# A graph layer and a slice-attention layer: identity matmuls added to TensorE's block loop

## The reference, cut to what matters

```python
# x: 6250 x 256; 106250 edges sorted by dst; all float32
edge_index = jnp.stack([src, dst])
# 1. graph layer on layernorm(x), 256 -> 256
support = x @ W
r_D = jax.nn.sigmoid(support @ a2)
gated = r_D * support
out = segment_sum(gated[col] * edge_values[:, None], row)     # row = src, col = dst
sumnorm = segment_sum(edge_values * r_D[col, 0], row)
out = out / sumnorm[:, None]
out = elu(max(out, 0) + softplus(out @ a1) * min(out, 0))
x = x + out
# 2. slice attention on layernorm(x), 8 heads, 64 slices of 64 channels
slice_weights = softmax((x_mid @ W_slice + b_slice) / temp)    # per node and head, over 64 slices
slice_token = einsum('bhnc,bhng->bhgc', fx_mid, slice_weights) / (slice_norm + 1e-5)
out_slice = softmax(q @ k.T * SCALE) @ v                       # tiny: 64 tokens per head
out_x = einsum('bhgc,bhng->bhnc', out_slice, slice_weights)
x = x + (out_x @ W_out + b_out)
```

## Time and profile before

| what | value |
|---|---|
| time, median of 3 runs | 1913.37 us (1912.43 to 1913.96) |
| time of the profiled execution | 1912.43 us |
| its span | 1910.5 us |
| PE busy | 1414.9 us (74%) |
| DVE busy | 1096.4 us (57%) |
| POOL busy | 902.8 us (47%) |
| ACT busy | 310.4 us (16%) |
| mean granted TensorE clock | 0.771 of full speed |

### The profile page before, as it was taken

How to read it: one execution, slowest core, us unless ns; L and a number is a source line. 1 busy time by engine, 2 the same in 40 slices (tenths; PEclk the granted TensorE clock), 3 DMA queues, 4 the chain that set the end, 5 groups by cost and what they waited for, 6 DMA issues and landing times.

```text
span 1910.5 us, 24715 instructions
## 1 busy us (share of the span) xinstructions
PE 1414.9 (74%) x6339; PEld 1032.4 (54%) x6340; DVE 1096.4 (57%) x2743; ACT 310.4 (16%) x800; POOL 902.8 (47%) x922
## 2 busy tenths in 40 slices
PE   4488877776588776777677876677776787777898
PEld 3477777775255444544445554445544454445687
DVE  8999999996344545444444454444444444444422
ACT  0022222222001111111111111111111111111133
POOL 0121111111666666666666666666666666665000
PEclk8688888887677777777777777677777777777899
DMA  7000000002633333333333333333333333333012
GB/s 205 2 22 20 20 20 20 20 20 34 103 94 86 88 82 86 88 85 88 88 85 91 88 85 86 88 90 88 85 85 86 90 87 86 92 84 84 26 63 71
DMA packets 92334, 139.42 MB, mean 73 GB/s; under 512 B 43147, under 2 KB 63007, under 8 KB 92312
## 3 DMA queue, kind: packets, MB, share of 16 engines
q0 software_dynamic: 42800, 114.46, 22.5%
q1 hardware_dynamic: 49512, 24.69, 4.8%
HBM read 123.65 MB, written 15.43 MB: 73 GB/s over the span
## 4 chain that ended last, share of the span: by engine, by line
PE 28%; issue 28%; DVE 26%; DVEq 6%; ACT 4%; another core or an unknown queue 3%; DMA 2%; POOL 1%; SPq 1%; ACTq 0%; POOLq 0%
PE bank L1261 27%; DVE big L667 6%; DVE big L677 5%; DVE S L932 3%; DVEq L82 1%; DVEq L932 1%; POOL rows L590 1%; DMA res<-in_x_dram 1%; DVE big L686 1%; PE bank L1310 1%; DVE big L656 1%; ACT xn L1203 1%; DVE lg L980 1%; ACT neg L1196 1%
## 5 line engine op out<-in xcount | busy, mean ns | idle before, releaser
L590 POOL DMA_INDIRECT rows<-gated_rows_dram,ring_i x857 | 825.6, 963 | 468.5 <-issue 228.4
L1261 PE MATMUL bank<-rows,S 128*128 128x257 f32 (+1 forms) x2156 | 621.0, 436 | 172.8 <-issue 159.0
L1261 PEld LDWEIGHTS bank<-rows,S 128*128 128x128 f32 x2156 | 464.1, 221 | 323.7 <-issue 237.4
L932 DVE TENSOR_SCALAR S<-iota,lof,srec 128x128 f32<-128x128 f32 x882 | 245.7, 359 | 101.0 <-issue 38.4
L1261 PE MATMUL bank<-big 128*98 128x80 f32 (+2 forms) x1741 | 220.0, 303 | 84.8 <-DVE big L699 84.8
L1261 PEld LDWEIGHTS bank<-big 128*98 128x98 f32 (+1 forms) x1741 | 215.3, 221 | 86.2 <-issue 86.2
L523 POOL DMA_INDIRECT sorted_edges_dram<-big,idx x52 | 74.8, 1439 | 389.4 <-ACT big L1114 278.3
L979 DVE TENSOR_REDUCE hm<-bank 128x8 f32<-128x512 f32 x49 | 33.9, 692 | 312.2 <-PE bank L1261 199.3
L1261 PE MATMUL bank<-Wxs,xT 128*128 128x512 f32 x196 | 181.1, 1079 | 5.2 <-ACT xT L1210 5.2
L1310 PE MATMUL bank<-ident,xn 128*128 128x128 f32 x98 | 32.0, 427 | 174.5 <-ACT xn L1203 141.0
L667 DVE TENSOR_TENSOR big<-big 128x784 f32<-128x784 bf16 x104 | 152.7, 1530 | 0.0
(11 more groups left out here) (209 smaller groups left out, 1217.3 us busy)
## 6 DMA issues: line engine op xcount, KB each, us to landing
rows<-gated_rows_dram,ring_i POOLq DMA_INDIRECT x857
gated_rows_dram<-S SPq DMA_DIRECT2D x49, 128.5 KB
res<-in_x_dram SPq DMA_DIRECT2D x1, 6144.0 KB
out_dram<-S SPq DMA_DIRECT2D x48, 128.0 KB, 1.7
sorted_edges_dram<-big SPq DMA_DIRECT2D x2, 465.5 KB, 7.2
sorted_edges_dram<-big,idx POOLq DMA_INDIRECT x52, 2.3
srec<-sorted_edges_dram SPq DMA_DIRECT2D x2, 374.0 KB
srec<-in_L_ffn_W_x_dram SPq DMA_DIRECT2D x2, 256.0 KB
```

Of the source, the lines that this page charges most:

```text
L590: pool.indirect_dma_start(rows[:, u, :], None, gtab[:, :], bass.IndirectOffsetOnAxis(ap=ring_i[:, k, u:u + 1], axis=0)).then_inc(s_row[u], 16)
L932: v.tensor_scalar(S[:, u, :], iota[:, :], lof[:, k, u:u + 1], srec[:, 1, ds(b * TQ + u, 1)], ALU.is_equal, ALU.mult).then_inc(s_S, 1)
L1261: return nc.tensor.matmul(o, l, r, start=start, stop=stop, skip_group_check=True)
```

## The change: identity matmuls in the block loop

A helper `idle(n)` is added in TensorE's program. It multiplies the identity by itself n times into columns 256 to 383 of `bank[6]`, with no wait and no semaphore. One such product follows each of the row tiles 4 to 9, and eight stand ahead of the transposes of each block but the last, which keeps its `spin(8)`. The first row tiles of block 0, which are done ahead of the loop, get the six too.

```diff
@@ segment(b, k, lo, hi, start=False)
                     mm(bank[k][:, 0:GW], S[:, u, :], rows[:, u, :], u == 0, u == TQ - 1).then_inc(s_seg, 1)
+                    if 4 <= u < 10:
+                        idle(1)
+
+            def idle(n):
+                for _ in range(n):
+                    mm(bank[6][:, F:F + P], ident[:, :], ident[:, :])
@@ main(b, k, left, start=False, second=False)
                 if left:
                     segment(b + 1, 1 - k, 4, 10)
-                if not left:
+                if left:
+                    idle(8)
+                else:
                     spin(8)
                 transposes(b + NB, xn[:, :], bank[6][:, 0:F])
```

## The result

| | before | changed |
|---|---|---|
| median, 4 runs each | 1913.66 us (1912.43 to 1916.32) | 2015.04 us (2006.90 to 2015.55) |
| ratio, 95% interval | | 1.0518 (1.0489 to 1.0547) |
| profiled span | 1910.5 us | 2004.9 us |
| mean granted clock | 0.771 | 0.826 |
| a pass of two blocks | 52.69 us | 56.56 us |

I had predicted 1864 us, faster. The clock came up as foreseen, and the kernel got slower all the same. The difference of the spans, 94.4 us, lies in the block loop. In the changed kernel the transposes of block 1 start at 562.08 and those of block 47 at 1863.05: 1300.97 us against 1211.91, 89 us more in 23 passes, and 9 more up to block 1, 4 less behind.

A forecast was written before the change was run, and what follows sets the result against it. TensorE's clock, falling in waits for `xn`, was taken to delay GpSimd's eleventh gather, with GpSimd's own time the floor. 80% of 2.55 us, 2.0 us x 24 passes = 49 us, gave 1864 us; range over the cases 1838 to 1935.

The forecast's parts named there:

- the clock behind the wait: TensorE behind the short block's wait for `xn`: windows would read 0.9 or more in place of 0.51.
- TensorE's wait for `xn`: Ahead of the transposes, 3.6 us each in 36 waits: the products would shrink it to under 1 us.
- the way to row tile 12: From the transposes through the logits: 4.69 us at full clock against 7.91, so 3.2 us less per block.
- the long block: Longer block of a pass: transposes 1.5 us late, row tile 14 done 2.2 us sooner, against 2.38 us to gain.
- the slow stretch: Long block until 1050.94, engines but GpSimd issuing slowly: bounded by time, so added products partly take row tiles' place in it.
- The last term: From `xn` to the transposes: 1.5 us late in the longer block, bounds 0 to 3.3; clock kept in the other.
- the short one: Shorter block of a pass: 3.3 us of products fit the 3.6 to 3.8 us wait at no cost.
- The floor: GpSimd's own time for a two-block pass: 50.14 us, 2.55 under today's 52.69.
- The other two: GpSimd's stops of 2.3 and 4.3 us at the starts of a pass's two blocks, taken as its own cost.
- D: Rival, chance 0.04: slow stretch goes by instructions at 0.70 us each, 14 us a pass, 336 us slower, 2249.
- A: Rival, chance 0.17: longer block's transposes 3.3 us late and cold, logits still 7.9 us, 79 us slower, 1992.
- C: Rival, chance 0.07: GpSimd's 4.3 and 2.3 us stops wait for TensorE; freed, 109 us faster, 1804.

The follow-up runs named there:

- e7: The changed kernel with the gathers of odd row tiles left out from block 1 on: 1645.2 us, 0.860 of the kernel before.
- e10: The changed kernel with all 14 products of a block cut to one row and one column, first kind of chip: 2023.9 us, 1.057 of the kernel before.
- e6: The kernel before with the gathers of odd row tiles left out from block 1 on: 1627.8 us, 0.851 of the kernel before.
- e11: The changed kernel with 7 products twice as wide in place of 14, first kind of chip: 1944.6 us, 1.016 of the kernel before.
- e16: The kernel before plus 14 products of 1x1 behind each block's last row tile: 2153.5 us, 1.135 of the kernel before.
- e5: The changed kernel itself on a chip of the second kind: 1695.5 us, 0.996 of the kernel before on that chip.
- e14: The kernel before without the products with `valid` in the slice sums, 16 TensorE instructions less a block: 1896.6 us, 1.000 of the kernel before.
- e13: The kernel before with a 2 us GpSimd pause ahead of tile 10 in the 18 gathers: 1925.0 us, 1.006 of the kernel before.
- e3: The changed kernel with all 14 products cut to one row and one column, second kind of chip: 1704.4 us, 0.999 of the kernel before.

## Why the prediction was wrong

**Right:** the clock behind the wait is up (0.771 to 0.826, logits' records 851 ns), the products take 0.12 us a record (18 in 2.17 us in e7), the transposes run at the upper level in 40 of 46 blocks (5 before), and TensorE's wait for `xn` is gone in 27 of 46. Where no signal is late, on a chip of the second kind, the way to row tile 12 is 4.05 us, even shorter than I had read from the earlier trace rows.

**The step that failed** is the one on the long block: "So I take the slow stretch as bounded by time, by GpSimd's gathers or what comes with them, and not by a number of TensorE's instructions." With that I priced the 56 added instructions at nothing but their array time. They cost as instructions: e10 has 5.7% without array time.

The mean block of the loop shows which terms of my sum that upset. It runs from one block's transposes to the next: the way to row tile 12, from there to the end of the next `xn`, and from `xn` to the next transposes. Before, it is 7.80 + 18.49 + 0.05, some 26.3 us; after, 8.13 + 18.50 + 1.66, some 28.3. I had put 3.2 us less on the first term. It came out 0.3 more: the copy of `xT` is 3.4 us later in the mean, because the signal of TensorE's transposes is late. That eats the clock's gain and lets the clock fall again. The last term is the lateness at the transposes, which I had at 1.5 us for the long block and at nothing for the short one: it is 1.6 us more in the mean of all blocks. So the lateness alone makes 1.6 of the 1.9 us that a block lost, and the gain that was to pay for it is gone.

**The floor was wrong too.** "The other two I take as GpSimd's own cost of a branch and a loop edge". They are gone on the second kind, in the changed kernel, where a pass takes 44.0 us. They are waits for TensorE's late signals, and the wait table had said so where I didn't believe it. The gather that starts at 1025.52 asks for row tile 4 of the block before: six signals of row tiles come in one bunch from 1024.72 to 1024.94, though the last record of theirs ends at 1022.40, and GpSimd's wait ends at 1024.77. The one at 1052.08 follows a bunch from 1051.28 to 1051.41. I had taken the record of a row tile for the moment at which GpSimd hears of it.

**The rivals.** D, with a chance of 0.04, was the right family, and its price of 336 us assumed each instruction at 0.70; 101 were measured. I gave it little because TensorE and VectorE leave the stretch together. That was the sign of a shared cause, and I read it as a sign that TensorE's own list doesn't matter. A, with 1992 us, came nearest to the measured 2015, in part by luck. Its lateness happened, 1.6 us in all blocks where it had 3.3 in the long ones. Its cold clock did not: the clock had risen in most blocks, and the logits' way was long because of the late signal. Nor is the lateness mainly the products' array time, as A had it: in e10, which has next to none, the transposes still come 1.0 us late. C was right about the stops, which are waits for TensorE, and wrong that TensorE would be sooner.

**Open.** Which path the engines and the gathers share isn't shown. It isn't a fetch of instructions that the trace would see. The DMA queue of instructions has 12 packets in 0.20 MB for the whole execution (11 and 0.18 before):

```profile
q8 instruction: 12, 0.20, 0.0%
```

and from 620 to 1870 us, nearly all of the loop, the gathers' queue is the only one in the list:

```profile
q0 software_dynamic: 36768, 100.84, 30.3%
```

Shown is that VectorE's slow stretch goes when nearly every second gather goes (e6), that the cost grows with TensorE's added instructions (e10, e11) and changes with their place in the block (e16), and that both the stretch and the late signals are absent on some chips (e5). TensorE's late signals do not need the stretch: e7 has them in 43 of 46 blocks without it. Why 16 instructions less give nothing (e14), why a 2 us pause doesn't help (e13), and what differs between the chips I can't say.

One rival is untested. Every time here comes with a span and a clock of its own, so it is the time of an execution that was recorded. On the first kind the record itself has holes: of VectorE's signals between 600 and 1500 us it has 854 for 1390 instructions that raise one (kernel before), on the second kind 1682 for 1683 (e5). If writing the record is what holds the engines up on these chips, each added instruction would cost there whatever it computes, as in e10. No run on record is without one, so this is neither shown nor excluded.

## What to carry to other kernels

Filling a wait of TensorE to keep its clock costs instructions, and where a trace shows engines that start one instruction each 0.7 or 1.4 us without a releaser, that may be the dearer coin: use few and wide products, or move work that is there already into the wait. When an engine whose program you don't change is suddenly late, look at what it waits for: here it answered within 0.02 us to a signal that came late from the engine that was changed. A record's end is not the moment at which the others hear of it. And a stall that several engines share and that the profile can't name is no constant of the kernel: before taking it as a floor, look whether another chip has it.

## What the runs showed of the hardware

- The same program (the kernel before) takes 1704 to 1706 us on two chips and 1898 to 1916 us on four. For the changed kernel both kinds have a trace, and the difference is nearly all in the block loop: a pass of 44.0 us (e5) against 56.6.
- On the four, semaphores that TensorE raises come microseconds behind the records of its instructions, in bunches some 0.04 us apart (346 of 634 late by over 0.06 us in the changed kernel, 339 of 614 before); on one of the two none of 898 does. The waiting engine starts 0.02 us behind the signal.
- On chips of the first kind, 56 tiny instructions a block cost 5.7% among row tiles 4 to 9 and ahead of the transposes (e10) and 13.5% at the end of the block (e16); on one of the second kind the first place has a ratio of 0.999 (e3).
- A product of one row and one column in float32 takes some 0.03 us a record (28 in 0.84 us in e16) where nothing holds it.
